# A Mamba block with an FFN on 8 cores: the decay tile dA in float32 with three buffers instead of float16 with four, and dbx with one buffer instead of four

## What is computed

```python
xz = einsum('bld,ed->ble', x, W_in); xc, z = split(xz, 2)
xc = silu(causal_conv1d(xc, conv_w) + conv_b)              # d_inner = 2048, 4 taps
xp = einsum('bld,ed->ble', xc, W_x)                        # B (16), C (16), dt (1)
delta = softplus(xp[..., -1:] * w_dt + b_dt)
A   = -exp(A_log)                                          # (2048, 16)
dA  = exp(delta[..., None] * A)
dBx = (delta * xc)[..., None] * B_in[:, :, None, :]
h_t = dA_t * h_{t-1} + dBx_t;   y_t = sum_n h_t[n] * C_t[n]
y = (y + D_param * xc) * silu(z);  out = y @ W_out.T
x = layernorm(x + out)                                     # then FFN, layernorm
```

## Time and profile before

| | us |
|---|---|
| median of two runs | 7940.26 (7912.84 to 7967.69) |
| the profiled execution, its own time | 7983.87 |
| its span on the slowest core (core 3), first to last instruction | 7980.9 |
| spans of the eight cores | 7896.3 to 7980.9 |
| DVE busy / ACT busy / PE busy, of that span | 4881.4 / 3233.1 / 3776.1 |
| stage A on core 3, first dbx to the last iteration's end | about 897 to 6190 |

### The profile page before, as it was taken

How to read it: one execution, slowest core, us unless ns; L and a number is a source line. 1 busy time by engine, 2 the same in 40 slices (tenths; PEclk the granted TensorE clock), 3 DMA queues, 4 the chain that set the end, 5 groups by cost and what they waited for, 6 DMA issues and landing times.

```text
span 7980.9 us, 68303 instructions; the slowest of 8 cores (7896.3 to 7980.9 us)
## 1 busy us (share of the span) xinstructions
PE 3776.1 (47%) x18720; PEld 1923.6 (24%) x18720; DVE 4881.4 (61%) x4777; ACT 3233.1 (41%) x8279; POOL 608.2 (8%) x514
## 2 busy tenths in 40 slices
PE   4445353252442524325244262442500588858888
PEld 2223232131221312213123041230300223222223
DVE  1000498898988989889889898898988000000000
ACT  4443354454544544455454454544532122212222
POOL 0010010000100001000010000100010000000000
PEclk9999676575665756757667566565755788777887
DMA  3576242231322313224232242322400322243332
GB/s 81 111 126 151 78 127 83 66 110 60 112 85 64 112 60 110 86 63 118 73 93 91 55 125 71 90 91 55 126 15 24 77 88 94 83 106 100 100 95 90
DMA packets 591441, 708.02 MB, mean 89 GB/s; under 512 B 421359, under 2 KB 421359, under 8 KB 552160
## 3 DMA queue, kind: packets, MB, share of 16 engines
q1 hardware_dynamic: 561024, 608.48, 25.3%
q0 software_dynamic: 30048, 95.17, 6.7%
HBM read 707.33 MB, written 71.84 MB: 98 GB/s over the span
## 4 chain that ended last, share of the span: by engine, by line
DVE 51%; PE 19%; ACT 7%; DMA 6%; issue 5%; DVEq 2%; another core or an unknown queue 1%; ACTq 0%; POOL 0%; POOLq 0%; SPq 0%
DVE hc L790 25%; DVE dbx L768 7%; PE ps_h L977 7%; DVE hc L800 6%; PE ps_oB L1009 4%; DMA w_r<-w2T_scr 4%; DVE hc L802 3%; PE ps_xz L586 3%; ACT dA L710 2%; DVE hc L804 2%; DMA w1s_r<-win1s_scr 2%; DVE gtmp L810 1%; DVE hc L806 1%; DVE ybuf L814 1%; PE ps_h L980 1%
## 5 line engine op out<-in xcount | busy, mean ns | idle before, releaser
L790 DVE TENSOR_TENSOR_SCAN hc<-dA,dbx 128x2048 bf16<-128x2048 f16 x512 | 2273.4, 4440 | 39.4 <-issue 2.3
L710 ACT ACTIVATE dA<-delta,a_sb 128x256 f16<-128x256 f32 x4096 | 1680.1, 495 | 1317.6 <-DVE hc L790 1312.4
L586 PE MATMUL ps_xz<-xT,w1s_r 128*128 128x256 bf16 x8192 | 1060.2, 293 | 405.9 <-ACT xc L663 259.9
L768 DVE TENSOR_TENSOR dbx<-vv,brep 128x2048 bf16<-128x2048 bf16 x512 | 630.9, 1232 | 741.0 <-POOLq L543 652.8
L379 PE MATMUL ps_wo<-wout_r,ybuf 128*128 128x512 bf16 x1024 | 409.7, 552 | 1270.6 <-DVE ybuf L814 971.1
L586 PEld LDWEIGHTS ps_xz<-xT,w1s_r 128*128 128x128 bf16 x8192 | 835.8, 104 | 601.9 <-issue 436.6
L571 PE MATMUL ps_tr<-ident,x_bf 128*128 128x128 bf16 x256 | 67.8, 265 | 1306.1 <-ACT xT L648 951.4
L540 POOL TENSOR_TENSOR vv<-delta,xc 128x256 bf16<-128x256 f32 x256 | 451.3, 1794 | 2797.0 <-ACT delta L697 2797.0
L602 PE MATMUL ps_xz<-xT,win_r 128*128 128x256 bf16 x2048 | 423.9, 388 | 421.2 <-ACT zsil L671 223.7
L800 DVE TENSOR_TENSOR hc<-hc,crep 128x4096 bf16<-128x4096 bf16 x256 | 598.2, 2337 | 20.2 <-issue 1.3
L1009 PE MATMUL ps_oB<-w_r,h_sb 128*128 128x512 bf16 x2048 | 538.6, 414 | 75.3 <-DMA w_r<-w2T_scr 61.1
(11 more groups left out here) (114 smaller groups left out, 3859.3 us busy)
## 6 DMA issues: line engine op xcount, KB each, us to landing
w1s_r<-win1s_scr SPq DMA_DIRECT2D x256, 1024.0 KB, 5.1
w_r<-w2T_scr SPq DMA_DIRECT2D x512, 256.0 KB, 3.1
win_r<-winT_scr SPq DMA_DIRECT2D x256, 256.0 KB, 3.0
wout_r<-woutT_scr SPq DMA_DIRECT2D x256, 256.0 KB, 2.7
win1s_scr<-p_stage SPq DMA_DIRECT2D x64, 256.0 KB, 2.4
brep<-bc_scr POOLq DMA_DIRECT2D x16, 1024.0 KB, 10.8
crep<-bc_scr POOLq DMA_DIRECT2D x16, 1024.0 KB, 15.3
out<-outsb SPq DMA_DIRECT2D x32, 512.0 KB, 3.5
```

The lines of the kernel that those rows point to most:

```text
L586: jx = t.matmul(pst[:], w1s_ring[jj % 2][:, (k4 * NKD + kt) * P:(k4 * NKD + kt + 1) * P], xT[par][:, kt * TE + 1 + k4:kt * TE + 1 + k4 + T ...
L710: jx = s.activation(da_t[:, n8 * T:(n8 + 1) * T], delta[dt % 8][:], AF.Exp, scale=a_sb[:, dt * NST + n:dt * NST + n + 1])
L768: jx = v.tensor_tensor(dbx[jh % 4][:].rearrange("p (n t) -> p n t", n=8), vv[par][:, dt * T:(dt + 1) * T].unsqueeze(1) .broadcast_to([P, 8 ...
L790: jx = v.tensor_tensor_scan(hc[:, nh * 8 * T:(nh + 1) * 8 * T], dA[jh % 4][:], dbx[jh % 4][:], 0.0, OP.mult, OP.add)
```

## The change

dA becomes float32 (it was float16) and has three buffers where it had four. ACT's wait moves with it: half jh is written once scan jh - 3 has finished. dbx has one buffer where it had four; all its users are on DVE. In bytes per partition, dA goes from 4 x 4096 to 3 x 8192 and dbx from 4 x 4096 to 4096. The rest is unchanged, the state hc and dbx stay bfloat16.

```diff
-    dA = [tsb(f"dA{j}", [P, 8 * T], FP16) for j in range(4)]
-    dbx = [tsb(f"dbx{j}", [P, 8 * T], BF16) for j in range(4)]
+    dA = [tsb(f"dA{j}", [P, 8 * T], F32) for j in range(3)]
+    dbx = [tsb(f"dbx{j}", [P, 8 * T], BF16) for j in range(1)]
...
             def emit_dA(i, dt):
                 for nh in range(2):
                     jh = (i * NDT + dt) * 2 + nh
-                    da_t = dA[jh % 4]
-                    if jh >= 4:
-                        ev.wait(s, f"scan_{jh - 4}")
+                    da_t = dA[jh % 3]
+                    if jh >= 3:
+                        ev.wait(s, f"scan_{jh - 3}")
...
                         jx = v.tensor_tensor(
-                            dbx[jh % 4][:].rearrange("p (n t) -> p n t", n=8),
+                            dbx[0][:].rearrange("p (n t) -> p n t", n=8),
...
-                                dA[jh % 4][:].rearrange("p (n t) -> p n t", n=8)[:, :, 0],
+                                dA[jh % 3][:].rearrange("p (n t) -> p n t", n=8)[:, :, 0],
...
-                        jx = v.memset(dA[jh % 4][:]
+                        jx = v.memset(dA[jh % 3][:]
...
                         jx = v.tensor_tensor_scan(hc[:, nh * 8 * T:(nh + 1) * 8 * T],
-                                                  dA[jh % 4][:], dbx[jh % 4][:],
+                                                  dA[jh % 3][:], dbx[0][:],
                                                   0.0, OP.mult, OP.add)
```

More of the change, by code:

```diff
@@ L783, in _ @@
                             jx = v.tensor_tensor(
-                                dbx[jh % 4][:].rearrange("p (n t) -> p n t", n=8)[:, :, 0],
-                                dbx[jh % 4][:].rearrange("p (n t) -> p n t", n=8)[:, :, 0],
+                                dbx[0][:].rearrange("p (n t) -> p n t", n=8)[:, :, 0],
+                                dbx[0][:].rearrange("p (n t) -> p n t", n=8)[:, :, 0],
                                 fixb[:, nh * 8:nh * 8 + 8], OP.add)
-                        jx = v.memset(dA[jh % 4][:]
+                        jx = v.memset(dA[jh % 3][:]
                                       .rearrange("p (n t) -> p n t", n=8)[:, :, 0:1], 0.0)
```

## The result

The changed kernel takes 8110.86 us in the median of 11 runs (8061.0 to 8156.04), beside 7987.44 us for the kernel before in 10 runs (7912.84 to 8016.47). The ratio is 1.0169, with a 95% interval from 1.0132 to 1.0206. It goes by the means of the runs, 135 us apart (1.7%); the medians are 123 us apart (1.5%). Forecast were 124 us, 1.6%, 8064 against the first two runs' median; that the measured 8110.86 lies 47 us above 8064 is the base, 7940.26 from two runs against 7987.44 from ten. Whether the loss is above 2% the interval leaves open. Some executions fall in a slower state, in which the cores of one die show a lower granted clock: all ratios here leave them out, the medians keep them.

A forecast was written before the change was run, and what follows sets the result against it. DVE was taken to bound stage A; a 13.05 us later start less about 4.8 spare gives 8.26 us in each of fifteen iterations, 124 us, on 7940 making 8064 us, with everything else at nothing; range 7990 to 8125.

The forecast's parts named there:

- What bounds the kernel: Stage A: DVE is the bound, 51% of the chain; ACT idles 1318 us before dA, but not at dt 6 to 12.
- The later start, 13.05 us: ACT's dA(6,1) must wait for scan(5,0) instead of scan(4,1), so it starts 13.05 us later.
- The train keeps its length: ACT's queue from dA(6,1) to dA(9), with evacuations and delta half, has no absorbing pause: all of it runs 13.05 us late.
- The price at dt = 8: DVE waits for vv's second half from POOL; dbx(8,0) starts 2.9 us late, at the other end 11.2.
- the rival built on 13.37: POOL's vv at dt = 8 keeps its 13.37 us although DVE waits: 168 us more, 8108 us; chance 0.14.
- The price at dt = 9: DVE waits for dA(9,0): 7.3 us late in iteration 5, including dt = 8's 2.9; about 8.26 us an iteration.
- spare times: Time between dA(9,0)'s first half being ready and dbx(9,0)'s start; mean 4.8 us, extremes 2.3 and 6.9, subtracted from 13.05.
- What stays hidden: At the iteration's end, bcsb and vv's first half stay covered, with 35.6 us to spare.
- The type: Float32 dA read by DVE's scan and written by ACT costs nothing; upper end 1.23 us a scan, 630 us in all.
- The rival with the slower scan: The float32 operand slows DVE's scan: up to 630 us more, 8570 us; chance 0.05.
- The catch-up: PE fills banks ahead and ACT's pauses shrink, leaving only 2.9 us at dt = 8: 44 us, 7984; chance 0.11.

The follow-up runs named there:

- e8_f16_six: Kernel before with six float16 buffers of dA in place of four, and one dbx buffer; 8001.2 us, ratio to the kernel before 1.0013.
- e3_f32_two: Changed kernel with two float32 buffers of dA in place of three; 8225.27 us, ratio to the kernel before 1.0337.
- e5_sched_four: Changed kernel with the 32 evacuations in eight groups of 4, not seven of 5 or 4, bcsb after dA(14); 7967.44 us, ratio to the kernel before 0.997.
- e2_f32_four: Changed kernel with four float32 buffers of dA in place of three, room made from small tiles; 7983.45 us, ratio to the kernel before 1.002.
- e1_f16_three: Changed kernel with dA back in float16, still three buffers and one dbx; 8120.86 us, ratio to the kernel before 1.0183.

## Why the prediction was right, point by point

- *What bounds the kernel.* Right: DVE paces stage A, and ACT's thousand idle microseconds did not hide the later start, since none of its waits for a scan lay in the train. e8_f16_six shows the other side: more lead gains nothing.
- *The later start, 13.05 us.* Right to the hundredth: the rows after have dA(6,1) 2679.58 - 2675.06 = 4.52 us behind the start of scan(5,0), those of before 2642.36 - 2633.83 = 8.53 us ahead of it, 13.05 apart. e3_f32_two moved it by another half-step, as counted.
- *The train keeps its length.* Right: 77.65 us for 78.17 in iteration 5, 79.65 for 79.70 in the mean of all iterations and cores. e5_sched_four, which shortened it by 15.4 in that mean, took the loss away. This is the strongest evidence for the mechanism.
- *The price at dt = 8.* The term of 2.9 us was too low. In iteration 5 the distance from dbx(7,0) to dbx(8,0) is 2738.12 - 2712.13 = 25.99, against 22.18 before, so 3.8 later; the mean of core 3 is 4.4. The train reached POOL 0.6 us later than forecast in the mean, and DVE started 0.46 after vv where I had put 0.2. So DVE waited 7.2 us before dbx(8,0) in the mean of core 3, where 5 to 6 were forecast. The choice of 5.05 us for vv on an idle DVE, rather than 13.37, was right to the digit, and the rival built on 13.37 falls.
- *The price at dt = 9.* Right in size: 3.8 at dt = 8 and 22.52 - 19.48 = 3.0 at dt = 9 make 6.8 in iteration 5, where 7.3 were forecast, and the fifteen iterations of core 3 make 7.9 where its own spare times gave 8.3. Over the eight cores an iteration grew by 8.4.
- *What stays hidden.* Right that nothing at the iteration's end is late. vv's first half fell from 15.6 to 7.1 us, which I had not foreseen, but DVE gains nothing by it: the groups dt = 14 and 15 together take 54.7 us before and after.
- *The type.* Right in the main: 4431 ns for 4440, and e2_f32_four 1.002. The rival with the slower scan falls. Put at nothing, the type gave DVE about 0.5 us an iteration, as e1 and e2 show; it is why core 3 loses 7.9 at dt 8 and 9 and 7.4 in all. The section "The perf-mode tier table" of the Trainium skill's page "VectorE: DVE Perf Modes" speaks of tensor_tensor, and the measured 4431 ns decide against carrying it over to the scan. The 8570 that the prediction put beside that rule was mis-sized: it is the price of one more pass at L768's pace, while a scan at half its pace would cost another 4.44 us each, 512 times, an estimate of 2270 us.
- *The catch-up.* Falls: PE's pauses moved with ACT.

That the sum agrees to a microsecond is in part luck. The 124 came from the spare times of one core, 4.7 us in the mean of its fifteen iterations (the prediction has 4.8); the mean of all eight cores was 4.2, which makes 13.05 - 4.2 = 8.9 us an iteration, and cores with less to spare lose up to 9.4. The 0.5 us that the type gives back, which the prediction had not seen, brings 8.9 to the 8.4 measured; e1_f16_three, without it, lost 8.9.

## What to carry to other kernels

A buffer count is a start time. To price a buffer less, find the last instruction it holds back before the producer's dense stretch, take the distance between the two releases as the shift, and subtract the spare time at each place where the consumer meets the end of that stretch; the producer's total idle time says nothing. A loss of this kind can be won back by shortening the stretch, without the memory. And removing the wait that a trace names can give nothing, if another item of the same late queue stands right behind it.

## What the runs showed of the hardware that was not expected

POOL's pace beside DVE depends on which DVE instruction it meets. The eight instructions of vv's first half took 15.6 us when they began inside a scan and the next scan ran over them whole (kernel before, e2_f32_four, e3_f32_two, float16 and float32 alike), 7.1 us in most iterations of the changed kernel and e1_f16_three, where they began in the adds behind a scan (up to 12.0 where they reached the next scan), and 5.05 us on an idle DVE. POOL's timeline of e3_f32_two, with float32, shows the slow case:

```profile
2923.44 15.60 POOL L540 TENSOR_TENSOR vv<-delta,xc 128x256 bf16<-128x256 f32 x8 [39.36 <-ACT delta L697]
```

DVE pays as well. In the slow case the scan beside it took 4.75 us, as in this row of the kernel before, beside the 15.60 of the earlier trace rows:

```profile
2828.06 4.75 DVE L790 TENSOR_TENSOR_SCAN hc<-dA,dbx 128x2048 bf16<-128x2048 f16 x1
```

The eight instructions taken singly show what the scan does: one that nothing delays lasts 0.66 us, and the one that started at 2828.49, 0.43 after this scan, lasted 4.78 and ended at 2833.27, 0.46 after the scan's end at 2832.81. So POOL all but stood still while the scan ran.

Here are the changed kernel's rows on core 3 in the middle case, where the adds L804 and L806 are stretched (0.69 and 0.42 us undisturbed) and the scan that follows is not, as vv ended at 2881.94:

```profile
2874.87 1.20 DVE L804 TENSOR_TENSOR hc<-hc 128x1024 bf16<-128x1024 bf16 x1
2876.15 0.73 DVE L806 TENSOR_TENSOR hc<-hc 128x512 bf16<-128x512 bf16 x1
...
2882.08 4.42 DVE L790 TENSOR_TENSOR_SCAN hc<-dA,dbx 128x2048 bf16<-128x2048 f32 x1
```

What in the scan holds POOL back was not tried. For DVE it made no difference where the first half fell: the groups dt = 14 and 15 together take 54.7 us with the 15.6 us vv and with the 7.1 us one (kernel before, changed kernel, e3_f32_two), some 2.3 us more than without any stretching. Where DVE was idle, as beside the second half in the changed kernel, POOL's work cost it nothing.
